# Two attentions and a routed MLP on one core: key tiles in another order, other load queues, keys stored once, and some vector steps moved

## The reference

```python
# layer 1: causal attention, 16 heads of 8, rotary positions
Q, K = rope(x @ Wq.T), rope(x @ Wk.T); V = x @ Wv.T
a = softmax(where(causal, Q @ K.T / sqrt(8), -inf)) @ V
x = layernorm(x + a @ Wo.T)
# layer 2: attention without a mask, then a routed MLP
h = layernorm(x) * w1 + b1
x = x + msa(h)                       # 16 heads of 8, all 2048 keys
xf = layernorm(x) * w2 + b2
one_hot = one_hot(argmax(xf @ gate_w + gate_b), 8)
x2 = x + sum_e one_hot[:, e] * (gelu(xf @ w1[e]) @ w2[e])   # hidden 512
out = layernorm(x2_in + x2)          # x2_in: the input of layer 2
```

## Time and profile before

| | |
|---|---|
| runs | 893.73, 896.61 and 900.15 us, median 896.61 |
| profiled execution | 894.7 us, span 893.0 us, mean granted TensorE clock 0.959 |
| PE | 809.2 us busy (91%) |
| ACT | 775.7 us busy (87%) |
| DVE | 328.5 us (37%) |
| POOL | 228.5 us (26%) |
| first scores on PE | at 33.31 us |

### The profile page before, as it was taken

The page is one execution under the profiler, slowest core; times in us unless marked ns, Lnnn a source line. Parts: engine busy times, 40 slices in busy tenths (PEclk is TensorE's granted clock), DMA queues, the critical chain, the costliest instruction groups (busy, mean ns, idle before and its releaser), DMA issues.

```text
span 893.0 us, 24266 instructions
## 1 busy us (share of the span) xinstructions
PE 809.2 (91%) x9940; PEld 369.5 (41%) x9952; DVE 328.5 (37%) x948; ACT 775.7 (87%) x906; POOL 228.5 (26%) x367
## 2 busy tenths in 40 slices
PE   8689999999999998999999999999999999996271
PEld 4244444444443443444344444444444444443240
DVE  5434525312430014320042433255332363334763
ACT  3579889999999998999999999999999899994440
POOL 5542211111110010000003343323334141443382
PEclk9799999999999999999999999999999999998575
DMA  8977220202110431810201000301000010001001
GB/s 273 269 210 224 96 49 2 95 2 49 49 48 1 108 84 40 244 50 3 48 2 32 1 3 3 78 8 37 3 3 19 14 43 3 1 3 31 30 14 41
DMA packets 34644, 51.60 MB, mean 58 GB/s; under 512 B 4064, under 2 KB 15072, under 8 KB 34528
## 3 DMA queue, kind: packets, MB, share of 16 engines
q1 hardware_dynamic: 32992, 46.30, 18.2%
q0 software_dynamic: 1536, 3.67, 1.3%
HBM read 29.12 MB, written 20.84 MB: 56 GB/s over the span
## 4 chain that ended last, share of the span: by engine, by line
PE 76%; DVE 8%; ACT 4%; issue 4%; DMA 2%; SPq 2%; POOL 2%; POOLq 1%; another core or an unknown queue 1%; DVEq 0%; ACTq 0%
PE ps L488 72%; ACT probs L922 3%; PE ps L493 3%; PE ps L787 1%; POOLq L1070 1%; DMA query_rows<-q_scratch 1%; POOL parts L1077 1%; DVE ln_newton L1156 1%; DMA q_scratch<-parts 1%; DVE q_rotated L1312 1%; DVE ln_newton L1155 1%; DVE z_rows L1176 1%; DVE ln_stats L1161 0%; DVE ln_newton L1154 0%
## 5 line engine op out<-in xcount | busy, mean ns | idle before, releaser
L922 ACT ACTIVATE probs<-ps 128x1024 f32<-128x1024 f32 (+3 forms) x832 | 736.0, 1017 | 41.5 <-PE ps L488 35.1
L488 PE MATMUL ps<-probs,values 128*9 128x256 f32 (+1 forms) x6528 | 426.3, 374 | 4.7 <-DVE q_rotated L1312 3.1
L488 PE MATMUL ps<-query_rows,key_rows 32*128 32x512 f32 (+3 forms) x1664 | 282.5, 485 | 17.5 <-ACT probs L922 10.2
L488 PEld LDWEIGHTS ps<-probs,values 128*9 128x9 f32 x6528 | 143.3, 90 | 182.5 <-issue 94.4
L488 PEld LDWEIGHTS ps<-query_rows,key_rows 32*128 32x128 f32 x1664 | 117.3, 183 | 183.5 <-issue 93.1
L1043 POOL TENSOR_SCALAR_AFFINE_SELECT probs<-probs 128x256 f32<-128x256 f32 x128 | 53.0, 420 | 234.4 <-ACT probs L922 231.5
L1090 POOL COPY parts<-early_late 128x512 f32 x63 | 44.5, 744 | 124.6 <-PE ps L488 124.6
L1048 POOL DMA_INDIRECT z_sorted<-z_rows,slot_numbers x16 | 15.8, 988 | 218.3 <-DVE slot_numbers L1447 208.8
L1312 DVE COPY q_rotated<-ps 128x512 f32<-128x512 f32 x30 | 20.7, 690 | 124.7 <-PE ps L488 124.6
L1077 POOL COPY parts<-parts 128x512 f32 x72 | 44.9, 663 | 29.3 <-PE ps L488 28.8
L1324 DVE RECIPROCAL recip<-ps 128x16 f32<-128x16 f32 x32 | 8.2, 256 | 70.5 <-PE ps L493 65.1
(11 more groups left out here) (184 smaller groups left out, 586.4 us busy)
## 6 DMA issues: line engine op xcount, KB each, us to landing
k_scratch<-parts SPq DMA_DIRECT2D x16, 512.0 KB, 3.9
q_scratch<-parts SPq DMA_DIRECT2D x16, 512.0 KB, 5.5
query_rows<-q_scratch SPq DMA_DIRECT2D x32, 256.0 KB, 5.3
key_rows<-k_scratch SPq DMA_DIRECT2D x20, 256.0 KB, 4.6
key_rows<-k_scratch SPq DMA_DIRECT2D x16, 192.0 KB, 4.5
parts<-in_w SPq DMA_DIRECT2D x1, 2048.0 KB, 8.9
early_late<-in_w SPq DMA_DIRECT2D x8, 256.0 KB, 8.0
early_late<-z_sorted SPq DMA_DIRECT2D x4, 384.0 KB, 3.1
```

What stands on the lines that cost most here:

```text
L488: return nc.tensor.matmul(out, l, r, start=start, stop=stop, skip_group_check=True)
L922: nc.scalar.activation(Pr[:, t % KEPT, 2 * p:2 * p + 2, lo:BLK], score_banks(t, p)[:, :, lo:BLK], ACT.Exp, bias=-SHIFT[r["a"]], scale=SCAL ...
```

## The change

- **Order of key tiles.** In causal quarters 1 to 3 the key tiles are taken in the order of a table; in quarters 2 and 3 the narrowest masked tile comes first, a full one stands behind each of the three narrow ones but the last, and the 2 x 512 one ends the run; in quarter 1 the widths are 2 x 256, 2 x 512, 2 x 128 and 2 x 384. Quarter 0 keeps its order. POOL's cuts follow.
- **Queues.** The small loads, and block 0's weights, go out on ACT's queue. SyncE has x transposed, cos and sin.
- **Keys stored once.** `k_scratch` loses its first dimension of parts; a store is one transfer. The loads read each row twice, with a broadcast dimension ahead of the rows. In block 0, group 0's rows of keys and queries are loaded first, each with semaphores of their own.
- **z.** `due(13)` becomes `due(PREP_AT[b][0] - 1)`, which is 13 in the blocks where the first entry is 14, and 12 where it is 13, the block before the second attention.
- **Gathers.** Their pace is 4, 6, 8 and 10 steps rather than 1 to 4.
- **Root.** One step of third order and one Newton step take the place of three Newton steps; in `normalize` the cubic one stands before `between()`, for z before the `due`.
- **Routing.** The one-hot tile comes from a reduction by maximum and compares; a second reduction over `first_wins` (8, 7, ... 1) keeps the first of equal ones; the sums are in pairs.
- **Start.** Block 0's keys and queries are rotated before `blk` is waited for and cast.

```diff
--- before.py
+++ after.py
...
 BOUND2_AT, OK2_AT = 38, 42
+ORDER = (
+    (0, 1, 2, 3),
+    (0, 1, 2, 3, 6, 4, 7, 5),
+    (0, 1, 2, 3, 4, 5, 11, 6, 10, 7, 9, 8),
+    (0, 1, 2, 3, 4, 5, 6, 7, 8, 15, 9, 14, 10, 13, 11, 12),
+)
 def steps_of(causal, qb):
...
         y_sorted = nc.dram_tensor("y_sorted", (SORTED, D), F32, kind="Internal").ap()
-        k_scratch = nc.dram_tensor("k_scratch", (2, NP, NP, DK, H, S), F32, kind="Internal").ap()
+        k_scratch = nc.dram_tensor("k_scratch", (2, NP, DK, H, S), F32, kind="Internal").ap()
         q_scratch = nc.dram_tensor("q_scratch", (2, NP, NP, DK, H, S), F32, kind="Internal").ap()
...
         def run_step(r, n):
-            causal, kt = r["a"] == 1, r["k0"] + n
+            causal = r["a"] == 1
+            order = ORDER[r["qb"]] if causal else range(r["k0"], r["k1"])
+            kt = order[n]
             cut = causal and kt >= r["qb"] * TB
-            done = sum(TB for q in RUNS[:r["n"]] if q["a"] == 1)
+            done = r["n"] * TB + sum(k >= r["qb"] * TB for k in order[:n])
             return dict(r=r, t=r["t0"] + n, kt=kt, lo=(kt % TB) * P if cut else 0,
-                        cut=2 * (done + kt % TB) + 1 if cut else None, start=n == 0, stop=kt == r["k1"] - 1)
+                        cut=2 * done + 1 if cut else None, start=n == 0, stop=n == len(order) - 1)
...
                 sp.dma_start(xT[:, c], xT_d[:, c]).then_inc(ld_t[b], 16)
-                if b == 0:
-                    sp.dma_start(wa[:, 2 * D:4 * D], wa_d[:, 2 * D:4 * D]).then_inc(ld_a, 16)
                 sp.dma_start(cos[:, c], cos_d[:, c]).then_inc(ld_b[b], 16)
                 sp.dma_start(sin[:, c], sin_d[:, c]).then_inc(ld_b[b], 16)
-                if b == 0:
-                    for w in (slice(0, 2 * D), slice(4 * D, 5 * D)):
-                        sp.dma_start(wa[:, w], wa_d[:, w]).then_inc(ld_q, 16)
-                    for t, s in ((blkf, blk_d), (ident, ident_d)):
-                        sp.dma_start(t[:, :], s).then_inc(ld_w, 16)
             def keys_out(a, b):
 -                for i in range(NP):
-                    sp.dma_start(k_scratch[a - 1, i, :, :, :, b * BLK:(b + 1) * BLK].rearrange("j d h t -> (d h) j t"),
-                                 k3[:, b]).then_inc(k_out[b], 16)
+                sp.dma_start(k_scratch[a - 1, :, :, :, b * BLK:(b + 1) * BLK].rearrange("j d h t -> (d h) j t"),
+                             k3[:, b]).then_inc(k_out[b], 16)
...
                                  q3[:, b]).then_inc(q_out[b], 16)
-            def rows_in(rows, scratch, a, g0, g1, t0, t1, done):
-                src = scratch[a - 1].rearrange("i j d (g f) t -> f (i j d) g t", f=HG)
+            def key_rows_in(a, g0, g1, t0, t1, done):
+                src = k_scratch[a - 1].rearrange("j d (g f) t -> f (j d) g t", f=HG)
                 for f in range(HG):
-                    sp.dma_start(rows[f * ROWS:(f + 1) * ROWS], src[f, :, g0:g1, t0:t1]).then_inc(done, 16)
-            def first_key_rows(b):
-                sp.wait_ge(k_out[b], 32)
-                rows_in(kaf[:, :, b * BLK:(b + 1) * BLK], k_scratch, 1, 0, G, b * BLK, (b + 1) * BLK, k_rows[b])
+                    sp.dma_start(kaf[f * ROWS:(f + 1) * ROWS, g0:g1, t0:t1],
+                                 src[f, :, g0:g1, t0:t1].unsqueeze(0).to_broadcast([NP, NP * DK, g1 - g0, t1 - t0])).then_inc(done, 16)
+            def query_rows_in(a, b, g0, g1, done):
+                src = q_scratch[a - 1].rearrange("i j d (g f) t -> f (i j d) g t", f=HG)
+                for f in range(HG):
+                    sp.dma_start(qaf[f * ROWS:(f + 1) * ROWS, b % 2, g0:g1],
+                                 src[f, :, g0:g1, b * BLK:(b + 1) * BLK]).then_inc(done, 16)
+            def key_rows(b):
+                sp.wait_ge(k_out[b], 16)
+                key_rows_in(1, 0, G, b * BLK, (b + 1) * BLK, k_rows[b])
             def query_rows(a, b):
                 sp.wait_ge(q_out[b], 32 * a)
-                rows_in(qaf[:, b % 2], q_scratch, a, 0, G, b * BLK, (b + 1) * BLK, q_rows[b % 2])
-            for t, s in ((wo, wo_d), (wqkv, wqkv_d), (wproj, wproj_d), (gw, gw_d), (iota, iota_d), (gb, gb_d)):
-                sp.dma_start(t[:, :], s).then_inc(ld_e, 16)
-            for n, s in enumerate((ln1w_d, ln1b_d, ln2w_d, ln2b_d)):
-                sp.dma_start(ln[:, n:n + 1], s).then_inc(ld_e, 16)
-            sp.dma_start(kc[:, :], kc_d).then_inc(ld_k, 16)
+                query_rows_in(a, b, 0, G, q_rows[b % 2])
+            def first_rows():
+                sp.wait_ge(k_out[0], 16)
+                key_rows_in(1, 0, 1, 0, BLK, k_first)
+                sp.wait_ge(q_out[0], 32)
+                query_rows_in(1, 0, 0, 1, q_first)
+                for g in range(1, G):
+                    key_rows_in(1, g, g + 1, 0, BLK, k_rows[0])
+                query_rows_in(1, 0, 1, G, q_rows[0])
             keys_out(1, 0)
             queries_out(1, 0)
-            first_key_rows(0)
-            query_rows(1, 0)
+            first_rows()
             keys_out(1, 1)
             queries_out(1, 1)
-            first_key_rows(1)
+            key_rows(1)
             query_rows(1, 1)
             keys_out(1, 2)
-            first_key_rows(2)
+            key_rows(2)
             keys_out(1, 3)
-            first_key_rows(3)
+            key_rows(3)
             queries_out(1, 2)
...
             for b in range(NB - 1):
-                sp.wait_ge(k_out[b], 64)
+                sp.wait_ge(k_out[b], 32)
             sp.wait_ge(gen_passed, NB)
...
                 sp.wait_ge(S_set, 2 * (r["t0"] + S // P))
-                rows_in(kaf[:, g:g + 1, 0:OLD * P], k_scratch, 2, g, g + 1, 0, OLD * P, k_early[g])
+                key_rows_in(2, g, g + 1, 0, OLD * P, k_early[g])
             query_rows(2, 1)
             keys_out(2, NB - 1)
-            sp.wait_ge(k_out[NB - 1], 64)
-            rows_in(kaf[:, :, OLD * P:S], k_scratch, 2, 0, G, OLD * P, S, k_late)
+            sp.wait_ge(k_out[NB - 1], 32)
+            key_rows_in(2, 0, G, OLD * P, S, k_late)
             queries_out(2, NB - 1)
...
             def keys_there(r):
+                if r["n"] == 0:
+                    pe.wait_ge(k_first, RDMA)
+                    pe.wait_ge(q_first, RDMA)
+                    return
+                if r["opens"]:
+                    pe.wait_ge(q_rows[r["qb"] % 2], RDMA * (2 * (r["a"] - 1) + r["qb"] // 2 + 1))
                 if r["a"] == 1:
-                    pe.wait_ge(k_rows[r["qb"]], RDMA)
+                    pe.wait_ge(k_rows[r["qb"]], RDMA if r["qb"] else 3 * RDMA)
                 elif r["qb"] == 0:
...
                                      scale=float(np.sqrt(2.0 / np.pi) * 0.044715)).then_inc(m_tanh, 1)
+            nc.scalar.dma_start(wa[:, 2 * D:4 * D], wa_d[:, 2 * D:4 * D]).then_inc(ld_a, 16)
+            for w in (slice(0, 2 * D), slice(4 * D, 5 * D)):
+                nc.scalar.dma_start(wa[:, w], wa_d[:, w]).then_inc(ld_q, 16)
+            for t, s in ((blkf, blk_d), (ident, ident_d)):
+                nc.scalar.dma_start(t[:, :], s).then_inc(ld_w, 16)
             act.wait_ge(dch, 1)
             nc.scalar.activation(gen_rec[:, :], onesf[:, 0:1], ACT.Exp)
+            for t, s in ((wo, wo_d), (wqkv, wqkv_d), (wproj, wproj_d), (gw, gw_d), (iota, iota_d), (gb, gb_d)):
+                nc.scalar.dma_start(t[:, :], s).then_inc(ld_e, 16)
+            for n, s in enumerate((ln1w_d, ln1b_d, ln2w_d, ln2b_d)):
+                nc.scalar.dma_start(ln[:, n:n + 1], s).then_inc(ld_e, 16)
+            nc.scalar.dma_start(kc[:, :], kc_d).then_inc(ld_k, 16)
             act.wait_ge(init, 2)
...
                     for n in range(NB):
-                        pool.wait_ge(k_out[n], 64)
+                        pool.wait_ge(k_out[n], 32)
                 for r in range(ROUNDS):
...
                     if b < NB - 2:
-                        pace(first_step(2, b + 2) + 1 + i)
+                        pace(first_step(2, b + 2) + 4 + 2 * i)
                     nc.gpsimd.indirect_dma_start(out=yback[:, i, :], out_offset=None, in_=y_sorted,
...
                 for r in runs_in(1, qb):
-                    for i in range(TB):
-                        cut(run_step(r, qb * TB + i))
+                    for n, kt in enumerate(ORDER[qb]):
+                        if kt >= qb * TB:
+                            cut(run_step(r, n))
                     if r["n"] == 0:
...
                 newton(y, h, t, turns)
+            def root_start(y, h, c, var, v):
+                ts(c, var, CUBIC, CUBIC * EPS, ALU.mult, ALU.add)
+                ts(h, var, -0.5, -0.5 * EPS, ALU.mult, ALU.add)
+                link(ts(y.bitcast(I32), v.bitcast(I32), -0.5, 1597463007.0, ALU.mult, ALU.add))
+            def cubic(y, c, t, u):
+                link(tt(t, y, y, ALU.mult))
+                link(tt(t, t, c, ALU.mult))
+                link(nc.vector.scalar_tensor_tensor(out=u, in0=t, scalar=-1.25 / CUBIC, in1=t, op0=ALU.add, op1=ALU.mult))
```

(72 more changed lines are left out.)

2 lines of the change are left out of this document (1 added, 1 removed).

## The result

The changed kernel takes 975.63 us (median of 4 runs, 974.69 to 976.88), the one before 895.17 (4 runs, 891.32 to 900.15): a ratio of 1.0896, 95% interval 1.0838 to 1.0955. It is 80 us slower, where 876 was forecast. The profiled execution has a span of 972.7 us, 79.7 more than before.

What follows compares the result with a forecast made beforehand. The prediction took ACT to pace the two long attention stages, so its idle time is lost time. Terms of 6.2+2.0+4.0+2.0+2.3+1.7+0.8+1.6 = 20.6 us gave 876 us; own range 867 to 887, extended to 970.

Steps and rivals of the forecast that it cites:

- key loads with two copies: Loads of keys with a two-copy broadcast: taken to last as the present key loads, 256 KB in 1.1 to 1.3 us.
- order, quarters 2 and 3: Narrow key tiles between full ones: 0.6 us saved in six quieter runs, 1.3 in two with side work, 6.2 together.
- order, quarter 1: New order of key tiles in the last two runs of quarter 1, where ACT's idle is longer: 2.0 us saved.
- start: First scores at 28.7 rather than 33.3; gain limited by the wait for residual rows x: 4.0 us, bounds 2 and 6.5.
- z of block 0: Block 0's z, late at present, comes sooner by two root steps less and a fuller tile: 2.0 us.
- z ahead of the copy of sums: Block before the second attention: z made ahead of the copy removes ACT's idle of 2.29 us: 2.3 us saved.
- gathers apart: Spacing the back-to-back gathers that delay DVE's reciprocal in quarters 2 and 3: 1.7 us saved, bounds 0 to 2.5.
- root in the route norms: Shorter root chain, 0.27 us each, at three route norms for which PE waits: 0.8 us saved.
- tail: Tail's routing instructions 1.1 us shorter, two norms on the path 0.5: 1.6 us saved.
- The rival: Two-copy key loads carried by two engines, x landing at 123 and late keys costing 24 us: 951 us, chance 0.43.
- x lands 4.3 us earlier: At the start, residual rows x land at 73.5 rather than 77.8, which sets the start's gain of 4.0 us.
- the start gives nothing: Rival: PE idles some 4 us for x in quarter 1, then gets half its clock: 882 us, chance 0.08.

Runs made afterwards that it cites:

- e5_x_early: Changed kernel with keys stored twice and loaded without broadcast, plus the x load moved ahead of the third block's key store: 880.74 us, ratio 0.9855.
- e6_before_x: Kernel before with only the x load moved ahead of the third block's key store: 893.67 us, ratio 1.0005.
- e1_twice: Changed kernel with keys stored twice again and loaded without a broadcast, all else kept: 886.64 us, ratio 0.9938.
- e8_root: Kernel before with only the cubic root step and the routing by reductions: 892.18 us, ratio 0.9974.
- e11_gathers: e5_x_early with the gathers' old pace (1 to 4 instead of 4 to 10): 880.28 us, ratio 0.9842.
- e3_inner: Changed kernel with the key loads' broadcast as second count, outermost 16, key and query loads one per group and head: 914.89 us, ratio 1.0246.
- e4_copies: Changed kernel with keys stored once but each copy loaded by a transfer of its own: 897.7 us, ratio 1.006.
- e12_run_order: e5_x_early with the plain order of key tiles in one run, the second group of quarter 2: 879.57 us, ratio 0.9843.
- e9_order: Kernel before with only the new order of key tiles and the gathers' new pace: 892.74 us, ratio 0.9988.
- e2_once: Kernel before with only keys stored once and loaded with a leading broadcast of two copies: 982.0 us, ratio 1.0994.
- e10_after_x: Changed kernel with only the x load moved ahead of the third block's key store: 941.59 us, ratio 1.053.
- e13: e5_x_early with the start as before (all loads on SyncE's queue, all groups' rows at once, blk cast before rotation): 882.6 us, ratio 0.9862.

## Why the prediction was wrong, step by step

The times in this table are from the starts of runs in the traces, in us saved. The last column has the changed kernel's parts where nothing hides them, in e5_x_early against e6_before_x unless another is named.

| step | forecast | measured |
|---|---|---|
| key loads with two copies | 0 | -88.8 (e1_twice against changed) |
| order, quarters 2 and 3 | 6.2 | 2.5 (the group of 21.65 left out, see below) |
| order, quarter 1 | 2.0 | 0.5 |
| start | 4.0 | 3.8; in e1_twice -2.8 at the third group of quarter 1 |
| z of block 0 | 2.0 | 0.5 (e8_root) |
| z ahead of the copy of sums | 2.3 | 3.7 |
| gathers apart | 1.7 | 0 (e11_gathers) |
| root in the route norms | 0.8 | 1.4 (e8_root) |
| tail | 1.6 | 2.6 (1.6 in e8_root; executions with the same tail differ by 1.6) |

**The key loads.** The step that failed is "I take the first: same bytes, same packets and same destination rows". The rows could not tell the two values apart, and I chose the one of the nearest rows, although these rows differ in just what the change changed, the outermost count. So the term stood at 0 and measured 89 us. e3_inner settles it: same bytes, same zero stride, outermost count 16, and all engines are busy. With the rule of the Trainium skill (DMA: Bandwidth & Descriptors, Rules for kernel authors), that a leading broadcast of c copies confines a transfer to at most c engines, the trace agrees, with 12.5% of sixteen engines. The rival had this mechanism, at a chance of 0.43.

**The rival's size.** It gave 951 and was 25 short. x was added at 138 rather than landing at 123: the sum had the two engines always busy, but a block's key store now takes 14.9 us to land (the one issued at 91.03, beside two busy engines), and the next loads wait for it. The late keys cost 28 us of wait and 1.2 in the short run behind it, where I had 24. And the 10.2 for order and z that I took off came to 3.5. This makes 27, of which the larger gain at the other z takes 1.4 back.

**The start.** First scores near 28.7 were right: ACT's first exponential comes at 29.7 to 30.7 in the eight kernels with the new start, at 33.6 to 34.5 in the five that have the old one and no slow loads. "x lands 4.3 us earlier" failed as well. In e1_twice x went out at 68.41, 1.2 later, since the second block's store is issued 4.5 us later than before, behind the first block's rows (the forecast had 3.9), and its key rows 1.7 later (37.17 instead of 35.46), where the forecast had them 0.5 earlier. The 3 x 1.3 us of the halved stores cannot show there, since e1_twice stores twice. In e4_copies they do (1.8 and 2.2 us in two blocks), but no run has them without more issues or slower loads. The rival "the start gives nothing" was right in its mechanism, idle PE and half clock behind it. So the start is worth 3.6 to 3.8 us, and needs x earlier.

**The order.** In four quiet runs it saves what was worked out, 0.6: 20.50 to 19.99 and 19.92 in quarter 2, 27.84 to 27.21 and 27.31 in quarter 3. The extra for runs with side work was wrong: the two first groups save 0.1 and 0.8, the second ones lose 0.6 and 0.0 (22.40 to 22.96, 28.72 to 28.76). The cause of the 0.6 is not the order within that run (e12_run_order), nor the faster start: e9_order, with the old one, has 22.94. PE waits 0.32 us for z there, which it didn't; that this wait makes the 0.6 is argued, not shown. Quarter 1 saved 0.4 in its first run and 0.1 in the last two together, where I had 2.0. Its second run saved 0.4 as well, but there e8_root, without the order, is the fastest (14.42 against 14.53), so this is the root's.

The table leaves out one thing. In three of the four undisturbed traces with the old order one group or two of quarters 2 and 3 take 1.1 to 1.4 us longer than their like: the first of quarter 2 in the kernel before (22.27 against 21.13), the third in e6_before_x (21.65 against 20.50), the second and the first of quarter 3 in e8_root (23.81 and 30.20 against 22.40 and 29.04). e2_once has none, and of the ten traces with the new order only e10_after_x has one, right behind its wait for query rows. The new order may be worth that much more; what these idle times come from is open.

**z.** Right in kind, and larger: beside the 2.29 us of the earlier trace rows, e6_before_x and e8_root have a second wait in this run, of 1.35 and 1.23 us, which the profiled execution of before lacked. Both are gone in e5_x_early, and as forecast z is made (332.37) ahead of the copy of sums (336.84):

```profile
332.37 0.87 DVE L1404 TENSOR_SCALAR z_rows<-x_rows,ln_newton 128x128 f32<-128x128 f32 x4
336.84 0.69 DVE L1364 COPY sums_so_far<-ps 128x512 f32<-128x512 f32 x1 [3.60 <-PE ps L505]
```

**The gathers.** The step "ACT loses 1.16 us in quarter 2 and 1.45 in quarter 3" took two waits of one execution for the kernel's. In e6_before_x, with the same code there, these groups take 30.90 and 30.91 us instead of 31.62 and 32.49, and e11_gathers shows nothing to save.

## What to carry to other kernels

Before a transfer is given a broadcast, look at its outermost count: one of 2 kept it to as much as two of sixteen engines here, one of 16 did not, and everything behind it in the queue, however unrelated, was late too. Where the rows can't exclude the worst bound and it costs many times what the part is to gain (here 54 us against the 4 of the halved stores), try that part alone first. A saved start is worth something only as far as the next latecomer; find it first and move it (here one line, 7.4 us). And before a wait of 1 us is booked as a gain, look for it in a second execution.

## What the runs showed that I had not expected

Quarter 0 differs from one profiled execution to another: its second group takes 6.80 us in e1, e5, e6 and e12, and 10.02 in e9, e11 and e13. In e11_gathers the granted clock is 0.50 from 39 to 49 us, where e5_x_early has 0.81 and 1.00, with code that is the same up to there; why, no run shows:

```profile
39.00:44.00 5.00, 4.67 (x48) 2.22 (x48) 3.06 (x15) 4.42 (x6) 2.44 (x7) 0.50 0.99 233
44.00:49.00 5.00, 5.00 (x38) 2.29 (x30) 2.02 (x9) 0.66 (x2) 2.20 (x4) 0.50 1.08 222
```

So 3 us of the difference between two spans may be this alone, and the single parts were judged from their own stages.

The time of an issue depends on what is on its way, too: SyncE took 0.62 us for a key load before (2.48 for four) and 2.5 us while the slow loads ran (10.07 for four).
